# A two-stage attention and feed-forward kernel: join of its stages, shifts by DMA, a shorter root, another order

## The reference, cut to what matters

```python
x = x + ga * attention(layernorm(x) * (1 + ca) + sa)   # stage A: 8 heads of 128, causal, rope
h = layernorm(x) * (1 + cb) + sb
for i in range(6):                                     # stage B, six layers
    h = attn_layer(shift_tokens(h)) + h
    h = ffn_layer(shift_tokens(h)) + h
x = x + gb * h

def shift_tokens(t):                                   # upper half of the width comes from the token before
    a, s = split(t, 2, -1)
    return concatenate([a, pad(s, one token in front)[:, :-1]], -1)

def attn_layer(x):      # 16 heads of 64
    q, k, v = split(x @ Wqkv, 3)
    q, k = l2norm(q) * qs, l2norm(k) * ks              # l2norm: t / max(norm(t), 1e-12) over the 64 of a head
    q, k = rotary with a scale by position
    out = softmax(8 * q @ k^T + mask) @ v              # windows of 32 tokens, each with the window before it
    return out @ Wo

def ffn_layer(x):
    xn = layernorm(x) * g + b
    a, gate = split(xn @ W1 + b1, 2)                   # 341 wide each
    return a * gelu(gate) @ W2 + b2
```

## Time and profile before

| | |
|---|---|
| median of 3 runs | 1872.73 us (1865.93 to 1878.46) |
| the profiled execution | 1868.75 us |
| its span, first to last instruction | 1867.0 us |
| mean granted TensorE clock | 0.983 of full speed |

### The profile page before, as it was taken

How to read it: one execution, slowest core, us unless ns; L and a number is a source line. 1 busy time by engine, 2 the same in 40 slices (tenths; PEclk the granted TensorE clock), 3 DMA queues, 4 the chain that set the end, 5 groups by cost and what they waited for, 6 DMA issues and landing times. The chain is left out here.

```text
span 1867.0 us, 66200 instructions
## 1 busy us (share of the span) xinstructions
PE 1732.8 (93%) x26984; PEld 1428.9 (77%) x26985; DVE 1472.2 (79%) x2952; ACT 1404.0 (75%) x2772; POOL 1479.4 (79%) x1830
## 2 busy tenths in 40 slices
PE   6999967899999999999999999999999999999985
PEld 4788755777778888787887787877778877888773
DVE  5878847778977888888879787888888798889752
ACT  3777744678877888878877877888788878788862
POOL 3777757779888887988888879789888888898860
PEclk9999988999999999999999999999999999999998
DMA  4000011111121111111110211112111101110100
GB/s 140 1 1 1 1 36 34 31 44 32 31 68 44 33 43 32 58 44 42 44 32 22 68 44 43 31 33 67 40 37 44 32 22 41 38 50 22 37 27 23
DMA packets 45485, 70.67 MB, mean 38 GB/s; under 512 B 15476, under 2 KB 28928, under 8 KB 45184
## 3 DMA queue, kind: packets, MB, share of 16 engines
q1 hardware_dynamic: 43712, 64.34, 11.8%
q10 hardware_dynamic: 1472, 2.10, 0.3%
HBM read 21.33 MB, written 1.05 MB: 12 GB/s over the span
## 5 line engine op out<-in xcount | busy, mean ns | idle before, releaser
L1087 POOL TENSOR_TENSOR ra<-ra,rb 128x512 f32<-128x512 f32 x384 | 492.3, 1288 | 116.7 <-DVE rb L1083 111.6
L1132 POOL TENSOR_TENSOR qn<-ra,rs 128x512 f32<-128x512 f32 x384 | 401.3, 1058 | 7.2 <-POOL rs L1125 0.8
L1062 DVE TENSOR_REDUCE ss<-sq 128x8 f32<-128x512 f32 x384 | 260.4, 678 | 91.2 <-ACT sq L1051 91.2
L1214 POOL TENSOR_TENSOR sp<-sp,rl 128x512 f32<-128x512 f32 x192 | 200.0, 1046 | 61.7 <-DVE rl L1209 61.0
L1201 ACT ACTIVATE sp<-sp 128x512 f32<-128x512 f32 x192 | 121.7, 634 | 38.5 <-DVE sp L1196 38.1
L1205 DVE TENSOR_REDUCE sm<-sp 128x8 f32<-128x512 f32 x192 | 128.6, 670 | 15.5 <-ACT sp L1201 13.0
L1179 PE MATMUL pP<-kT,qT 64*32 64x64 f32 x4608 | 106.9, 226 | 2.8 <-issue 2.2
L1179 PEld LDWEIGHTS pP<-kT,qT 64*32 64x32 f32 x4608 | 93.8, 105 | 16.3 <-ACT kT L1152 11.0
L489 POOL TENSOR_TENSOR ra<-ra,rb 128x512 f32<-128x512 f32 x64 | 81.5, 1288 | 29.6 <-DVE rb L485 29.6
L1190 DVE TENSOR_REDUCE mx<-pS 128x8 f32<-128x512 f32 x48 | 32.9, 685 | 91.2 <-PE pP L1179 91.2
L1083 DVE TENSOR_TENSOR rb<-pQ,rope 128x512 f32<-128x512 f32 x144 | 97.9, 680 | 2.9 <-POOL ra L1087 2.9
(11 more groups left out here) (355 smaller groups left out, 6194.3 us busy)
## 6 DMA issues: line engine op xcount, KB each, us to landing
vs<-v SPq DMA_DIRECT2D x96, 384.0 KB, 3.3
wqkvA<-in_L_ffn_Wqkv SPq DMA_DIRECT2D x18, 512.0 KB, 5.6
vs<-v SPq DMA_DIRECT2D x96, 64.0 KB, 3.0
woB<-in_L_ffn_Wo SPq DMA_DIRECT2D x6, 512.0 KB, 4.2
w<-in_L_ffn_W SPq DMA_DIRECT2D x6, 341.0 KB, 2.9
out<-x SPq DMA_DIRECT2D x4, 256.0 KB, 2.3
x<-in_L_attn_x SPq DMA_DIRECT2D x1, 768.0 KB, 8.1
w<-in_L_ffn_W SPq DMA_DIRECT2D x12, 64.0 KB
```

The source lines that it names most:

```text
L1062: e.tensor_reduce(ss[:, j, :], sq[:, j % 2, :].rearrange("p (h d) -> p h d", d=DB), AX.X, ALU.add).then_inc(b_ss.sem, 1)
L1087: e.tensor_tensor(ra[:, j, :], ra[:, j, :], rb[:, j % 2, :], ALU.add).then_inc(b_ad.sem, 1)
L1132: e.tensor_tensor(qn[:, j % 4, :].rearrange("p (h d) -> p h d", d=DB), ra[:, j, :].rearrange("p (h d) -> p h d", d=DB), rs[:, c % 2, 8 * j ...
L1214: e.tensor_tensor(y, y, rl[:, u, :].unsqueeze(2).to_broadcast([P, 8, 64]), ALU.mult).then_inc(b_pn.sem, 1)
```

## The change

The barrier, `mark_written` and the passes that drain stage A are gone. Stage A's list ends with batch 7's own pass, and four new lists, `join_pe`, `join_act`, `join_dve`, `join_pool`, hold what is left of batches 6 and 7 and all of stage B's first pair, mixed by hand; `stream` begins with pair 1. The token shift in `xt_turn` becomes a shift of columns in the copies behind two plain flips. `l_shift` becomes three DMAs on SyncE. The root takes nine steps, 0 to 4 on GpSimd, 5 to 8 on VectorE. The lists of a pair have a new order: both chunks' `xt_turn` at its start, and all of chunk c + 1 behind its projections (turns, scores, softmax, values) in the next pass; `l_stats` moves to the next pass, `m_add` comes earlier in its pass. `finish` of a quarter runs in the last layer two passes behind. All banks of stage B are drawn anew.

```diff
-NORM = 12
-ROOM = (1024.0 / 27.0) ** 2
+EVEN = 112
+NORM, FIT = 9, 5
+SERIES = (1.0, -0.49999832, 0.37500061, -0.3139403, 0.27406215)
+ROOM = 1.0 / SERIES[4] ** 2
+HORNER = [x / SERIES[4] for x in SERIES[3::-1]]
...
         def first_attention(e, batch):
-            for b in range(B + A_LAG):
-                batch(e, b, lambda q: 0 <= q < B)
+            for b in range(B):
+                batch(e, b, lambda q: q >= 0)
...
-            e.matmul(o[hi, 0:P], xc[:, 0, hi], down, start=True, stop=True)
-            e.matmul(o[hi, P:T], xc[:, 1, hi], down, start=True, stop=False, skip_group_check=True)
-            e.matmul(o[hi, P:T], xc[:, 0, hi], wrap, start=False, stop=True, skip_group_check=True)\
-             .then_inc(b_xt.sem, 1)
+            for t in range(NT):
+                i = flip(e, o, t, xr[:, (c % B) * NT + t, :])
+            i.then_inc(b_xt.sem, 1)
+
+        def shifted(l, c, x_):
+            o = xt_bank(l, c)
+            return ((x_[0:HALF, c % 2, :], o[0:HALF, 0:T]), (x_[HALF:M, c % 2, 1:T], o[HALF:M, 0:T - 1]))
...
-            e.copy(xsh[:, c % 2, :], banks[XT_BANK[c % 2]][:, 0:T]).then_inc(b_xh.sem, 1)
+            for dst, o in shifted(l, c, xsh):
+                i = e.copy(dst, o)
+            i.then_inc(b_xh.sem, 1)
```

(`xt_low` becomes two subtractions in the same way.) The root's steps from 2 on:

```diff
-            elif n in (2, 8):
+            elif n == 2:
                 e.tensor_tensor(t, y, x_, ALU.mult).then_inc(b_rs.sem, 1)
-            elif n in (3, 9):
+            elif n == 3:
                 e.tensor_tensor(t, t, y, ALU.mult).then_inc(b_rs.sem, 1)
             elif n == 4:
-                e.tensor_scalar(p, t, -10.0 / 3.0, None, ALU.add).then_inc(b_rs.sem, 1)
...
+                e.tensor_scalar(t, t, -1.0, None, ALU.add).then_inc(b_rs.sem, 1)
+            elif n == FIT:
+                e.scalar_tensor_tensor(p, t, HORNER[0], t, ALU.add, ALU.mult).then_inc(b_rs.sem, 1)
+            elif n < NORM - 1:
+                e.scalar_tensor_tensor(p, p, HORNER[n - FIT], t, ALU.add, ALU.mult).then_inc(b_rs.sem, 1)
             else:
                 e.wait_ge(b_qn.sem, b_qn.at(it - 2, QK - 1))
-                e.tensor_tensor(rs[:, c % 2, :], t, y, ALU.mult).then_inc(b_rs.sem, 1)
+                e.scalar_tensor_tensor(rs[:, c % 2, :], p, HORNER[n - FIT], y, ALU.add, ALU.mult).then_inc(b_rs.sem, 1)
```

The shift of the feed-forward's input, and `l_first`, now on ScalarE:

```diff
         def l_shift(e, l, q):
-            e.wait_ge(b_wx.sem, b_wx.at(l * B + 2 * q + 1))
-            o = banks[SHIFT_BANK]
-            e.matmul(o[:, 0:FT * HALF], down, xr[:, tiles(q), HALF:M], start=True, stop=False, skip_group_check=True)
...
+            it = l * FP + q
+            e.wait_ge(b_wx.sem, b_wx.at(l * B + 2 * q + 1))
+            e.sem_inc(e_hold.sem, 1)
+            e.wait_ge(f_ln.sem, f_ln.at(it - 1))
+            e.sem_inc(e_hold.sem, 1)
+            k = (q % FP) * FT
+            e.dma_start(fx[0:1, 1::NT, HALF:M], xr[P - 1:P, k:k + FT:NT, HALF:M]).then_inc(f_xs.sem, 16)
+            for lo, hi in ((EVEN, P - 1), (0, EVEN)):
+                e.dma_start(fx[lo + 1:hi + 1, :, :], xr[lo:hi, k:k + FT, :]).then_inc(f_xs.sem, 16)
...
         def l_first(e, l, q):
             it = l * FP + q
             e.wait_ge(b_wx.sem, b_wx.at(l * B + 2 * q + 1))
-            e.sem_inc(e_hold.sem, 1)
-            e.wait_ge(f_ln.sem, f_ln.at(it - 1))
-            e.sem_inc(e_hold.sem, 1)
-            e.tensor_copy(fx[:, :, 0:HALF], xr[:, tiles(q), 0:HALF]).then_inc(f_xa.sem, 1)
+            e.wait_ge(f_xs.sem, f_xs.at(it))
+            e.copy(fx[:, :, 0:HALF], xr[:, tiles(q), 0:HALF]).then_inc(f_xa.sem, 1)
```

More of the change, by code:

```diff
@@ L1152, in turn_copy @@
             e.copy(dst, w.rearrange("p (h q) -> p h q", h=4)).then_inc(b_tc.sem, 1)
-        def mark_written(e):
-            for n in SCORE_BANKS:
-                e.matmul(banks[n], ident16[:, :], maskB[:, :], start=True, stop=True)
         def mask(e, l, c, u):
@@ new lines, in pair_pe @@
+            if on(p):
+                proj(e, l, c, 4)
+            if on(p - 1):
+                scores(e, l, c - 1, 0)
+            if on(p):
+                e.wait_ge(b_ab.sem, b_ab.at(l * B + c, 1))
+            if on(p - 1) and not on(p):
+                e.wait_ge(b_ev.sem, b_ev.at(l * B + c - 1, 1))
+            if on(p - 1):
+                turn(e, l, c - 1, 5)
+                e.wait_ge(b_tc.sem, b_tc.at(l * B + c - 1, 3))
+                turn(e, l, c - 1, 6)
+                e.wait_ge(b_tc.sem, b_tc.at(l * B + c - 1, 4))
@@ L1499, in pair_pe @@
+            if on(p):
+                turn(e, l, c, 0)
             if on(p - 1):
                 e.wait_ge(b_oc.sem, b_oc.at(l * B + c - 1, 1))
+            if on(p) and not on(p - 1) and not on(p - 1):
+                e.wait_ge(b_ab.sem, b_ab.at(l * B + c, 4))
             if on(p):
-                xt_turn(e, l, c + 1)
-                e.wait_ge(b_ev.sem, b_ev.at(l * B + c, 1))
+                turn(e, l, c, 1)
+            if on(p - 2):
+                e.wait_ge(f_G.sem, f_G.at(l * FP + p - 2, 2))
@@ new lines, in pair_pe @@
+            if on(p):
+                turn(e, l, c, 5)
+                e.wait_ge(b_ab.sem, b_ab.at(l * B + c + 1, 2))
+                turn(e, l, c, 6)
+                e.wait_ge(b_tc.sem, b_tc.at(l * B + c, 4))
+                proj(e, l, c + 1, 3)
+                e.wait_ge(b_sub.sem, b_sub.at(l * B + c, 0))
+                turn(e, l, c, 7)
+                e.wait_ge(b_tc.sem, b_tc.at(l * B + c, 5))
+            if on(p - 1) and on(p - 2) and not on(p):
+                e.wait_ge(f_x.sem, f_x.at(l * FP + p - 2, 0))
@@ L1867, in pair_dve @@
                 square_sum(e, l, c + 1, 1)
+                rotate_cos(e, l, c + 1, 1)
+                rotate_sin(e, l, c + 1, 1)
+                square_sum(e, l, c + 1, 2)
             if on(p) and last(p):
@@ L2025, in stream @@
+        def stream(e, pair, after=lambda p: None):
+            for p in range(1, FP):
                 pair(e, 0, p, lambda q: q >= 0)
```

1273 lines of the change are left out of this document (830 added, 443 removed).

## The result

The changed kernel took 1882.4 us in the median of 15 runs (1877.4 to 1888.3, one at 2345), the kernel before 1869.6 (1865.9 to 1878.5): ratio 1.0061, interval 1.0047 to 1.0075. It is slower by 0.6%, which is inside the 1% that the forecast counts as no change. The run at 2345 us is slow and left out of the ratio. The forecast was 1777 with a range of 1735 to 1834. The profiled execution's span is 1883.0.

The account below looks back on a forecast made before the run. TensorE, 93% busy, was taken to bound the kernel. Pair 1's start 313, 23 periods of 61.0 (1403), drain 59 and 1.75 around the span gave 1777 us, 4.9% below 1868.75; range 1735 to 1834.

Parts of the forecast that it names:

- The period: Time per pair in the 23 pairs from pair 1: from 63.45 to 61.0 us, bounds 59.5 and 62.3.
- the work term: Within each pair: TensorE loses 1.9 us of work (xt_turn 1.2, l_shift 0.7) and 0.5 us of idle.
- 63.45 - 1.9 = 61.5: Pair period less TensorE's saved work, before a further 0.5 us of idle is taken off to reach 61.0.
- rival A: Period stays: less TensorE work buys no time because its busy time may be overstated; 1833 us, chance 0.20.
- The start of pair 1: Joined end of batches and pair 0: pair 1 starts at 313 us instead of 339.4, bounds 303 and 325.
- The drain: From the last pair's program end on TensorE to the finish: 59 us instead of 68.3, bounds 52 and 68.
- Rival C: Token shift's DMA lands late: ScalarE stands 1.5 us per pair at l_first, period 62.5; 1811 us, chance 0.12.
- Rival D: Root's hand-over from GpSimd binds VectorE: period 67.5 us, 1926 us in all, slower; chance 0.05.
- Rival B: Order packs better, GpSimd's short root ending most idle: period 59.5, start 308, drain 56; 1734 us, chance 0.11.
- the busy times of VectorE, ScalarE and GpSimd: Work per pair on these engines: about 55.8, 52.2 and 49.6 us, all below TensorE's 61.5.
- the cover of the shift: ScalarE's copies before l_first, 4.5 to 6 us, barely hide the shift DMA's about 4.8 us.
- slow end of 0.775: Root's new two-input VectorE steps: if slowed by GpSimd contention, 0.775 us each, 6.2 per pair rather than 2.8.

Follow-up runs that it names:

- before_shift_180: Kernel before with 90 tiny 32x8 matmuls (180 instructions with their weight loads) on TensorE between the barrier and mark_written, executed once: 1952.1 us, ratio 1.044.
- load_early: Changed kernel with load_ahead (the next layer's weight loads) moved back to the layer's start, nothing else: 1862.5 us, ratio 0.9949 to the kernel before.
- before_cuts: Kernel before, old order kept, with only TensorE's two cuts: xt_turn by flips and shifted copies, l_shift by DMA with l_first on ScalarE: 1936.2 us, ratio 1.0347.
- ffn_thin: Changed kernel with loads back at the layer's start, and second_layer and hidden-layer matmuls cut to 8 columns, same instructions: 1858.9 us, ratio 0.9946.
- root_on_vector: Changed kernel with loads back at the layer's start and all nine root steps on VectorE, none on GpSimd: 1852.8 us, ratio 0.9909.
- three drain runs: Changed kernel, loads at layer's start, last layer's third FFN pair made small on TensorE, ScalarE or both, in the remainder: 1866.7, 1864.6, 1869.3 us.

## Why the prediction was wrong

*The period* (61.0 forecast, 64.2) is the step that failed, by 70 of the 108 us. It had two terms. Late packets were not in it as such: before's 22.7 us in the 22 periods (1.0 each) lay unseen in 63.45 and were carried on, while the new order has 52.8 (2.4 each). That is 30 us. It is in part luck of placement: before_shift_180 shows that the kernel before could as well have had 77 us more. "The masks, turns, scores and values stay the same in number, only their banks and places move; I cost that at nothing" was wrong: their places in the stream cost 1.4 us per pair. "On SyncE itself the moved loads wait for things that come before ... 0 to 1 us per layer" was wrong too: the place of the loads costs 20 us in five layers (load_early), of which 16 are late packets and part of the 30 above; the rest goes with the lower clock in these pairs (0.93 for 1.00 in the one shown), which was not tried by itself.

The other 40 us are the work term. Without late packets the period fell from 62.5 to 61.8, 0.7 where 2.45 were forecast. The forecast had 1.9 less of TensorE's work and 0.5 less of idle; the windows have 1.1 less of busy time and, late packets aside, 0.4 more of idle (1.2 to 1.6). So both halves were mis-sized. Where 0.8 of the 1.9 went is open: `xt_turn` is cut to its flips and `l_shift` is gone as planned, and which other calls grew was not separated. "63.45 - 1.9 = 61.5" also took one us of TensorE's work for one us of time. before_cuts and ffn_thin show it isn't: idle and waits fill what the work leaves. The wait that appears is named in the trace, the flips of `qn` behind GpSimd's normalisation at the pair's start: 10.3, 9.0 and 1.6 us in their groups, 0.9 per pair, where before they had 4.7 and less, 0.3 per pair. That is more than the growth of the idle, where the forecast let it shrink. The rule of the Trainium skill (Perfetto Trace Analysis, Identifying the Most-Contended Engine) that stood beside rival A fits here as far as it went there: by weight loads TensorE is at 796.6 of 1032.7, 77%, behind VectorE's 86% and GpSimd's 78%, and its work was not what set the period. That VectorE was the bound instead is not shown: root_on_vector gives it 0.7 us more per pair and the pair stays.

*The start of pair 1* (313, came 328.6): VectorE's busy time was right (51.7 from 254.4 on, for 49), its standing was not (22.5 us for 10). Of it 8 us are square sums waiting for ScalarE's squares, which wait for projections; TensorE's clock is 0.77 at 275 to 290 and 0.87 over the part. How much of the rest is the clock wasn't tried.

*The drain* (59 forecast): `out_add` comes at 1850.7 in place of 1834, and from there to the end it is 32 for 28.8 (the drain's terms add up to 59.5, not 59.6). The last chunk's chain took 47 us for 30.7. GpSimd's last normalisation of `qn` ends at 1815.6, but its flips start at 1821.8 and the second `scores` call at 1827.7: ahead of them in TensorE's order stand `l_turn`, two calls of `out_proj` and the flips of the first softmax products, in part at half clock (matmuls 0.21 us apart where it is 0.11 at full):
```profile
1817.51 1.09 PE L336 MATMUL pO<-eye,early 128*128 128x128 f32 x4 [2.35 <-ACT early L1720]
1818.38 3.62 PE L1639 MATMUL pM<-woB,oT 128*128 128x128 f32 x16
1821.80 0.80 PE L336 MATMUL pP<-eye,qn 128*128 128x128 f32 x4
...
1823.29 1.95 PE L1639 MATMUL pM<-woB,oT 128*128 128x128 f32 x16
...
1827.65 0.21 PE L1550 MATMUL pT<-kT,qT 64*32 64x64 f32 x1 [0.26 <-ACT pP L1532]
```
The first line is `l_turn`, which waits 2.35 us for `l_norm`. The three drain runs exclude the FFN pair's matmuls and gelus; that `l_norm`, the fixed order ahead of the second `scores` and the clock make the rest is read from the timeline and was not tried.

*Rival C* fell: in all 24 pairs ScalarE stood 9.9 us for the shift, 9 of it in the last, in the drain. From `out_add` to the end of `l_first` it is 5.6 us there, for a forecast of 5.2.
```profile
L1684 ACT COPY fx<-xr x24: 404/451/455, 386.8 to 1855.9; 128x256 f32<-128x256 f32 x24
its engine sat idle before it (us, times) until:
  DMA fx<-xr: 9.9, 4
```
*Rival D* exists and is small: 38.3 us over the run, 1.6 per pair for a forecast of 2.4, and root_on_vector leaves the period as it is.
```profile
L1496 DVE SCALAR_TENSOR_TENSOR nt<-nt x48: 211/1280/1297, 290.5 to 1801.3; 128x64 f32<-128x64 f32 x48
its engine sat idle before it (us, times) until:
  POOL nt L1494: 38.3, 25
```
*Rival B* did not come: the changed kernel without late packets is 20 us better than the old one (1826 for 1845), not 130.

What was right: the busy times of VectorE, ScalarE and GpSimd, the cover of the shift, and within 3.5 us the length from the last `out_add` on. The join gains, but less than forecast: pair 1 starts 11 us earlier, not 26. In the profiled executions the kernel is 10.8 us shorter up to pair 1, without late packets 15.6 shorter in the 22 periods, and 12.3 longer from the last pair on; its 30 us more of late packets in these periods turn that into a loss of 16.

## What to carry to other kernels

Where an engine issues hundreds of small instructions back to back, look at "issue" idle inside a call, number its records, and see whether the stalls share one remainder by 256; a comparison of two orders is then also one of placements, worth up to 80 us here, and one run with a few instructions added ahead tells how much. Keep bulk loads away from such bursts. And don't price work taken from an engine that is 93% busy at its length: ask what is late next, and test it by making operations shorter with the stream unchanged.

## What was not expected of the hardware

- An instruction packet (16 KB, 256 instructions) is ready 2.5 us after its transfer starts; with DMAs 97% busy it started 6.8 us after the packet end that asks for it, where 1.1 is usual, and TensorE stood 6.7 us. Starts 7 to 9 us late also occur with idle DMAs: one at 606.5 for an end at 599.0, with a stall of 2.3 behind it, while the DMAs are 1% busy. Why, stays open.
```profile
596.00:605.00 9.00, 8.71 (x58) 6.88 (x56) 8.85 (x16) 8.93 (x17) 8.07 (x7) 1.00 0.01 0
```
- The root's first two-input step starts beside GpSimd's addition in 41 of 48 cases and then takes 0.8 to 1.30 us, ending some 0.08 us after that addition (1.28 us long); in the other 7 it takes 0.21, and the next three steps take 0.225 in every case. The forecast used 0.35 each and a slow end of 0.775; their sum per chunk, 0.97 in the mean + 3 x 0.225 = 1.6 us for 1.4, hid the error. The Trainium skill (GPSIMD Engine Reference, 1. Specifications) has the two contend for a shared interface, and the trace agrees for this one step; beside the next three no GpSimd instruction runs.
- A semaphore increment alone on TensorE takes 0.15 us, a 32x8 matmul with its load 0.025.
